# First attention: where the summed output of a step is scaled by the reciprocals

## The reference

```
q = einsum('bnd,hde->bhne', query, Wq) * scale       # k and v alike
attn = softmax(einsum('bhne,bhme->bhnm', q, k), axis=-1)
out = einsum('bhnm,bhme->bnhe', attn, v)             # 16 heads of 64
x = layernorm(x + swapaxes(out).reshape(...) @ Wp + bp)
```

## Time and profile before

| | |
|---|---|
| median of 3 runs | 1094.57 us (1093.62 to 1097.33) |
| profiled execution, its own time | 1092.86 us |
| its span, first to last instruction | 1091.1 us |
| TensorE busy in the span | 1031.3 us, 95% |
| VectorE | 836.5 us, 77% |
| GpSimd | 719.2 us, 66% |
| ScalarE | 638.2 us, 58% |
| mean granted clock of TensorE | 0.975 of 2.4 GHz |

### The profile page before, as it was taken

The page is one execution under the profiler, slowest core; times in us unless marked ns, Lnnn a source line. Parts: engine busy times, 40 slices in busy tenths (PEclk is TensorE's granted clock), DMA queues, the critical chain, the costliest instruction groups (busy, mean ns, idle before and its releaser), DMA issues. The chain is left out here.

```text
span 1091.1 us, 25198 instructions
## 1 busy us (share of the span) xinstructions
PE 1031.3 (95%) x7983; PEld 858.1 (79%) x7983; DVE 836.5 (77%) x1493; ACT 638.2 (58%) x1311; POOL 719.2 (66%) x736
## 2 busy tenths in 40 slices
PE   5889999999999999999999999887998799999996
PEld 4678888888888888888888888655686677777774
DVE  5977878878877877877877887656765589898896
ACT  4655655555556556556556565564443577666774
POOL 4167877877877877877877878611323387777772
PEclk9999999999999999999999999899899799999998
DMA  6143443543543543543543543110000012112111
GB/s 127 42 100 86 100 101 85 104 96 85 106 94 86 110 92 84 113 89 83 116 86 82 119 93 69 45 31 2 0 1 19 1 61 97 58 66 69 59 40 38
DMA packets 57041, 80.09 MB, mean 73 GB/s; under 512 B 25956, under 2 KB 38048, under 8 KB 55968
## 3 DMA queue, kind: packets, MB, share of 16 engines
q1 hardware_dynamic: 54792, 78.97, 31.7%
q10 hardware_dynamic: 2208, 0.59, 0.3%
HBM read 19.43 MB, written 1.11 MB: 19 GB/s over the span
## 5 line engine op out<-in xcount | busy, mean ns | idle before, releaser
L670 POOL TENSOR_TENSOR probs_lo<-probs 128x512 f16<-128x512 f32 x384 | 392.3, 1040 | 159.2 <-ACT probs L470 157.7
L470 ACT ACTIVATE probs<-bank_s 128x512 f32<-128x512 f32 x512 | 309.4, 605 | 263.1 <-PE bank_s L389 259.5
L511 DVE TENSOR_REDUCE maxes<-bank_m 128x1 f32<-128x512 f32 x512 | 353.1, 690 | 137.8 <-PE bank_m L301 128.5
L382 PE MATMUL bank_s<-qa,ka 128*128 128x512 f32 x512 | 228.4, 446 | 5.1 <-DVE arena L559 2.5
L301 PE MATMUL bank_m<-ka,qa 128*128 128x512 f32 x512 | 208.2, 407 | 3.4 <-DMA ka<-tk_lo 2.6
L389 PE MATMUL bank_s<-qb,kb 65*128 65x512 f32 x512 | 207.1, 404 | 0.9 <-DMA qb<-negmax 0.9
L324 PE MATMUL bank_o<-v_now,probs 128*128 128x129 f16 x2048 | 201.7, 221 | 0.3 <-ACT o_parts L436 0.3
L1386 POOL TENSOR_TENSOR hidden_lo<-rectified,hidden_hi 128x512 fp32r<-128x512 f32 x112 | 156.5, 1415 | 66.7 <-ACT hidden_hi L1558 56.6
L324 PEld LDWEIGHTS bank_o<-v_now,probs 128*128 128x128 bf16 x2048 | 176.2, 98 | 21.5 <-issue 20.4
L320 PE MATMUL bank_o<-v_now,probs_lo 128*128 128x65 f16 x2048 | 185.8, 193 | 0.0
L301 PEld LDWEIGHTS bank_m<-ka,qa 128*128 128x128 f32 x512 | 158.6, 310 | 31.5 <-issue 4.4
(11 more groups left out here) (271 smaller groups left out, 1704.0 us busy)
## 6 DMA issues: line engine op xcount, KB each, us to landing
qa<-tq_hi SPq DMA_DIRECT2D x64, 256.0 KB, 4.2
v_now<-arena SPq DMA_DIRECT2D x32, 260.0 KB, 2.3
ka<-tk_hi SPq DMA_DIRECT2D x32, 256.0 KB, 3.0
ka<-tk_lo SPq DMA_DIRECT2D x32, 256.0 KB, 5.1
kb<-tk_hi SPq DMA_DIRECT2D x32, 256.0 KB, 5.1
qb<-tq_lo SPq DMA_DIRECT2D x32, 256.0 KB, 5.2
gates_on_all<-gate_rows SPq DMA_DIRECT2D x8, 1024.0 KB, 4.6
e_raw<-in_L_ffn_ew_dram SPq DMA_DIRECT2D x16, 256.0 KB, 3.1
```

The lines of the kernel that those rows point to most:

```text
L382: nc.tensor.matmul(bank_s[u % 2][:], ka[h][:, ks], qa[h][:, qs], start=True, stop=False)
L470: nc.scalar.activation(probs[:, c, u, :], bank_s[u % 2][:], ACT.Exp, scale=SCALE).then_inc(exp_done, 1)
L511: nc.vector.tensor_reduce(maxes[:, j // 2, j % 2:j % 2 + 1], bank_m[j % 2][:], AX.X, ALU.max).then_inc(m_reduced, 1)
L670: nc.gpsimd.tensor_tensor(probs_lo[:, c, u, :], p, hi, ALU.subtract).then_inc(lo_pool, 1)
```

## The change

Line 645's multiplication moves from GpSimd to VectorE, as `scale_o`. GpSimd's `add_o` adds the halves and raises a new semaphore, `o_summed`, by 1. VectorE scales two units after it has inverted, at the end of unit 3, behind the low half of that unit; it waits for its own reciprocals and for `o_summed`, and raises `o_added` by 2, so all who wait for `o_added` wait for the same totals as before. The last two scalings of the last pair follow their `invert` on VectorE.

```diff
+            def scale_o(i, s):
+                h, c = s // 2, s % 2
+                o = o_pair[:, c, :, h * E:(h + 1) * E]
+                dve.wait_ge(rden_ready, 4 * i + s + 1)
+                dve.wait_ge(o_summed, 4 * i + s + 1)
+                nc.vector.tensor_tensor(o, o, rden[:, c, :].unsqueeze(2).broadcast_to((P, 4, E)), ALU.mult).then_inc(o_added, 2)
...
                     if u == INVERT_AT and not (first and s < 2):
                         bi, bs = (i, s - 2) if s >= 2 else (i - 1, s + 2)
                         invert(bi, bs, 8 * bi + 2 * bs + 2)
+                    if u == INVERT_AT + 2 and not (first and s < 2):
+                        bi, bs = (i, s - 2) if s >= 2 else (i - 1, s + 2)
+                        scale_o(bi, bs)
...
                 for bs in (2, 3):
                     invert(i, bs, 8 * i + 2 * bs + 2)
+                    scale_o(i, bs)
...
-                nc.gpsimd.tensor_tensor(o, o_parts[:, c, :, 0:E], o_parts[:, c, :, E + 1:P + 1], ALU.add).then_inc(o_added, 1)
-                pool.wait_ge(o_added, 8 * i + 2 * s + 5)
-                pool.wait_ge(rden_ready, 4 * i + s + 1)
-                nc.gpsimd.tensor_tensor(o, o, rden[:, c, :].unsqueeze(2).broadcast_to((P, 4, E)), ALU.mult).then_inc(o_added, 1)
+                nc.gpsimd.tensor_tensor(o, o_parts[:, c, :, 0:E], o_parts[:, c, :, E + 1:P + 1], ALU.add).then_inc(o_summed, 1)
```

More of the change, by code:

```diff
@@ L113, in attend_heads @@
         pv_done, rden_ready, o_taken, o_added = sem("pv_done"), sem("rden_ready"), sem("o_taken"), sem("o_added")
+        o_summed = sem("o_summed")
         raw_in = sem("weights_raw_in")
```

## The result

| | before | after |
|---|---|---|
| median of 4 runs, us | 1095.51 | 1113.18 |
| lowest and highest | 1093.62 to 1097.33 | 1111.3 to 1116.62 |
| profiled execution, its span | 1091.1 | 1109.5 |
| TensorE, VectorE, GpSimd busy | 1031.3, 836.5, 719.2 | 1038.3, 879.9, 694.2 |

The ratio is 1.0179, with a 95% interval of 1.0157 to 1.0201: 17 to 22 us slower. The two medians differ by 17.7 us, the ratio stands for 19.6. The forecast was 1113.5 us, from a sum of +18.9.

The account below looks back on a forecast made before the run. TensorE's list was taken to set the pace in the first attention. Terms of 10.8 + 6.2 + 0.7 + 1.4 - 0.2 = 18.9 us, added to 1094.57, gave 1113.5 us; own range 1108 to 1122, widened to 1099 to 1122 for a rival.

Parts of the forecast that it names:

- Step 0: Steps 4 to 60, 15 times: scaling waits at the port behind GpSimd's low half, transposes' loads 0.72 us later; 10.8 us.
- The scaling's own time: VectorE's 128x256 scaling, interpolated at 0.42 us, bounds 0.29 and 0.68; these shift the sum by -3.9 or +7.8 us.
- Step 1: Steps 5 to 57, 14 times: VectorE reaches the scaling after TensorE reaches the transposes; 0.44 us each, 6.2 us.
- Step 61: Has no projection and looks like a step 0: next scores at 678.2 instead of 677.47; 0.7 us.
- Step 3: 14 times: first reduction starts late and delays a weight load; 0.1 us each, bounds 0 and 0.25; 1.4 us.
- Step 2: ScalarE's copies in unit 4 start 0.22 us late; costed at nothing, 3.1 us if the cover were gone.
- The end: Last scaling on VectorE (0.42 us and a wait) replaces GpSimd's multiplication of 0.61; -0.2 us.
- VectorE keeping the port: Rival: in step 0 the scaling runs before GpSimd's waiting low half; +5.1 us, 1099.7 us; chance 0.12.
- More than the waits: Rival: TensorE's queue runs empty at each late transpose and refills; 5.1 us more, 1118.6 us; chance 0.08.
- No change: Rival: VectorE keeps the port and its release reaches TensorE at once; +1.7 us, 1096.3 us; chance 0.07.
- faster: Rival: in step 0 weight loads could start 0.24 us earlier, 3.6 us come back; 1091.0 us; chance 0.05.

Follow-up runs that it names:

- three split kernels: s0_only, s1_only and s23_only: the changed kernel with VectorE scaling in the named steps alone, GpSimd in the others; +10.6, +7.1 and +2.6 us over the kernel before.
- twice: Changed kernel with one more multiplication of the same size on VectorE ahead of each scaling, to a spare tile; 1135.41 us, 1.0369 of the kernel before.
- The gate: Changed kernel, but GpSimd waits after its addition until VectorE has scaled, then makes its low half of unit 2; 1100.36 us, 1.0058 of the kernel before.
- s23_only: Changed kernel with VectorE scaling only in steps 2 and 3 of each pair, GpSimd in the others; 1096.84 us, 1.0024 of the kernel before.
- before_late: Kernel before, with GpSimd's addition and multiplication at unit 2 instead of unit 1, behind its low half of unit 2; 1121.56 us, ratio 1.0245.
- s0_only: Changed kernel with VectorE scaling only in steps 0 (15 places), GpSimd in the others; 1104.73 us, 1.0097 of the kernel before.
- s1_only: Changed kernel with VectorE scaling only in steps 1 (14 in the loop and step 61); 1100.96 us, 1.0065 of the kernel before.
- gate_early: Changed kernel, scaling ahead of VectorE's low half of unit 3, and GpSimd waiting after its addition for the scaling; 1094.39 us, 1.0008 of the kernel before.
- add0_early: Changed kernel, scaling ahead of VectorE's low half of unit 3, GpSimd's addition at unit 0 instead of 1; 1094.97 us, 1.0006 of the kernel before.
- add0_before: Kernel before, with GpSimd's addition and multiplication at unit 0 instead of unit 1; 1092.34 us, ratio 0.9984.

## Why the prediction was right

**What bounds.** Right. Whatever makes TensorE late in this stretch is added to the time, shown by the three split kernels adding up and by `twice` in steps 0 and 1 (0.33 and 0.34 more).

**Step 0, 0.72 us x 15.** Right in size and cause: 0.71 measured (11.51 - 10.80). The order at the port was the weakest link, taken from 16 places in another stage; here GpSimd got in every time: the scaling lasts 1.25 or 1.26 us in all 36 steps 0, 2 and 3 of the 12 pairs, and 0.41 or 0.42 in the 12 steps 1. The gate took the loss away.

**The scaling's own time.** 0.42 interpolated, 0.41 to 0.42 measured where nothing blocks it.

**Step 1, 0.44 us x 14.** Right: 0.45 (12.44 - 11.99). VectorE's own low half did get its 0.42 back (0.68 instead of 1.10), and it isn't enough, since the scaling starts behind it.

**Step 61.** Right: forecast 0.7, and the interval from its fifth exponential to the sixth grew by 0.69 (1.15 to 1.84). Its period grew by 0.83 (10.54 to 11.37), but 0.15 of that lies ahead of the next step's scores, which waited for a late transfer of the row that had been issued at 697.1 us:

```profile
700.68 0.19 PEld L390 LDWEIGHTS bank_s<-qb,kb 65*128 65x128 f32 x1 [0.20 <-DMA qb<-negmax]
```

**Step 3, 0.1 us x 14.** Right, and in the way described: the first reduction frees a bank late, the load of line 302 comes about 0.24 late and the wait for the exponential behind it shrinks by 0.11 (means over 12 steps of the distance between score matmuls: 0.74 to 0.98, then 2.19 to 2.08). The bound of 0.25 came out, though the prediction's own numbers don't give it: a reduction 0.27 late with 0.08 to spare makes 0.19.

**Step 2, at nothing.** A small miss: it grew by 0.08, 14 times that is 1.1 us. s23_only shows the same 0.08, so it comes from the scalings of steps 2 and 3. It is ScalarE's copies, by the path of before_late: over the 12 steps the exponential behind them ends 0.22 later (5.87 to 6.09 from the step's first one), as forecast for the copies. The scores of unit 7 start at 6.17 before and after, but their second matmul comes at 6.48 instead of 6.40. The maximum matmuls ahead of them are later by at most 0.03, in s23_only too, so it isn't the reduction. So 0.14 of the lateness was covered, and not all of it.

**The end, -0.2.** Not seen: from the first exponential of step 63 to the end of the last scaling it is 15.76 us after and 15.74 before. In s0_only and s1_only, where step 63's own scaling stays on GpSimd and only the last two are VectorE's, it is 15.48. So the gain of 0.26 is there. That step 63's own scaling, a term that the forecast doesn't have, takes it back fits the 15.85 of s23_only, which has both too; it wasn't tested alone.

**The sum.** In the two profiled executions the 14 middle pairs, from step 4 to step 60, account for 18.8 us (569.55 to 588.34), steps 60 to 62 for 1.7, and the start of the attention for -2.3, which is no part of the change (below). Without the start and the late transfer in step 61 that is 20.3, which is also the sum of the three split kernels. The forecast of 18.9 is 1.4 under it: step 2 is missing with 1.1 and another 0.17 in step 62, and the -0.2 of the end didn't come. A pair grew by 1.34, with 1.2 forecast. That the median of 1113.18 lies 0.3 from the forecast is luck: the medians differ by less than the ratio says. The forecast's own range was also not quite its bounds: 7.8, 2.1 and 3.1 on top of 18.9 make 1126.5, not 1122.

**The rivals.** VectorE keeping the port is excluded by the 1.26 us. More than the waits: the queue running empty adds nothing, since in step 1, where it runs empty only after the change, the loss is what the late scaling alone gives. No change and faster both needed an earlier release; gate_early and add0_early have it, and come out as no change. Step 0 then gets 0.05 to 0.08 back (add0_before the most) and not the 0.24 that the last rival took for TensorE's own time. That nothing was to be won at this place is shown by them and by add0_before.

## What to carry to other kernels

Moving work to a faster engine is judged by the time at which its result is released in the list of the new engine, not by its own duration: 0.42 us instead of 0.61 made the result 0.72 and 1.5 us later. Where two engines share a port, look at who will be standing there between two back-to-back instructions. And if the move is wanted, move the place too: one unit earlier for the addition and ahead of the low half for the scaling made the whole loss disappear.

## What the runs showed of the hardware that was not expected

One transfer of 2 KB, the row of negated maxima, takes 1.9 us from issue to landing nearly every time. In 10 of the 12 kernels the one that is issued near 79 us of the span took 3.2 to 3.7 us, and the score matmul that needs it started 1.1 to 1.7 us late. A second late one (2.8 to 3.4 us) came near 331 to 350 us in six kernels, and another in the last three steps of most. In the kernel before, the line of the transfers' landing times over all 64, and in s1_only the one late matmul of the twelve pairs:

```profile
DMA to landing us min/median/max: 1.9/1.9/3.3
```

```profile
338.73 0.50 PE L391 MATMUL bank_s<-qb,kb 65*128 65x512 f32 x1 [0.80 <-DMA qb<-negmax]
```

The kernel before had such a landing for the row issued at 79.9 us, and the changed one had none there; that is about half of the -2.3 us at the start. What makes a transfer late stays open; it happens with and without the change. The rows for steps 3 and 0 have only 0.2 to 0.4 us between landing and use, so a late one there is paid nearly in full.

The other half is a step 1 of the first pair of 11.92 us before and 10.66 after, ahead of the first instruction that the change moves, and it goes with the order at the port. The two low halves there, before and then after:

```profile
61.48 1.04 POOL L670 TENSOR_TENSOR probs_lo<-probs 128x512 f16<-128x512 f32 x1 [1.90 <-ACT probs L470]
61.54 1.53 DVE L589 TENSOR_TENSOR probs_lo<-probs 128x512 f16<-128x512 f32 x1
```

```profile
61.22 0.68 DVE L597 TENSOR_TENSOR probs_lo<-probs 128x512 f16<-128x512 f32 x1
61.55 1.25 POOL L679 TENSOR_TENSOR probs_lo<-probs 128x512 f16<-128x512 f32 x1 [2.61 <-ACT probs L471]
```

Before, GpSimd comes 0.06 us ahead, VectorE's low half takes 1.53, and TensorE then waits 0.85 for the reduction behind it. In six of the twelve kernels it is so, and the third exponential of that step is followed by the fourth after 2.73 to 2.75 us; in the other six VectorE comes first, its low half takes 0.68, and the distance is 1.49 to 1.79. No experiment sets this order, and what decides it was not found. Kernels differ by 1.0 to 1.3 us in that step through it, without any part of the change.
